# An adaLN block on one core: prologue in another load order, last batch with second homes and its own PSUM banks

## The chip, the cores and the metric

The kernel runs on one core of one Trainium2 chip. The metric is device time in microseconds (us) of one execution; lower is better. Before the change it is 464.82 us, the median of three runs (464.0 to 464.89).

## The reference, cut to what matters

Four batches of 1,024 tokens, 512 wide. A conditioning vector makes six modulation vectors per batch; the block is an attention half and a feed-forward half.

```python
mod = (silu(c) @ wmod).reshape(4, 6, 1, -1)
sa, ca, ga, sb, cb, gb = [mod[:, i] for i in range(6)]      # ga, gb: sign * max(|.|, 0.25)
h = layernorm(x) * (1 + ca) + sa
scores = einsum('hr,bir,bjr->bhij', ones, h @ Wq.T, h @ Wk.T)   # the same for all 16 heads
x = x + ga * (softmax(scores) @ (h @ Wv.T)) @ Wo.T
h = layernorm(x) * (1 + cb) + sb
x = x + gb * (einsum('btd,rde->bte', h, factors) / sqrt(8) + bias)
```

All heads have the same scores, so the kernel multiplies Wv and Wo once into one 512x512 matrix ("wvo"), and sums the eight factors once.

## The kernel before, in words

The 4,096 tokens are 32 tiles of 128 (T = 32), eight per batch. Every product is made in three matmuls (`three`, L461): each operand is split by ScalarE (ACT) into a rounded "hi" part and by VectorE (DVE) into the rest, "lo". SB, CB and so on are the modulation vectors, each made by eight narrow matmuls from its 512x512 piece of `wmod` (`w_part` holds the pieces' parts).

**Prologue.** SP loads Wv, Wo, wmod in four row chunks k each; PE makes wvo (`weights_term`, `weights_last`), the vectors SA and CA between them, then projects the eight tiles of the first batch (`prep_pair`). PE begins with seven fp32 matmuls on zeros (WARMUPS, L672). `scores(0)` and `modulation_columns(1)` stand at the prologue's end.

**Steps.** `step(t)` on every engine handles tile t: PE turns or takes the turned softmax of tile t, projects tile t+8, makes the feed-forward of tile t-3 (`feed_forward`, 12 matmuls of 512 columns), the scores of tile t+2 (4 matmuls), and `attend(t)` (24 matmuls). All but a few tiles turn their softmax without PE: `send_p` writes it to DRAM, `fetch_p` reads it back in quarters, DVE transposes 32x32 blocks (`turn_p`), ACT makes `pt_hi` (`probs_part`), DVE `pt_lo` (`probs_rest`). This is called the P trip below. The normalised x1 goes the same way (`send_x1`, `fetch_x1`, `turn_x1`), then `modulate_x1`, `h2_upper` (ACT) and `h2_rest` (DVE) make the feed-forward's input. After it ACT copies the result out (`ffn_out`), GpSimd (POOL) adds bias, gates and adds it (`add_bias`, `gate_result`, `add_result`), and SP stores pairs of tiles.

**Order.** Every engine runs its own list in program order, and semaphores join them; a waiting instruction holds all behind it on its engine, SP's DMA issues too. The last eight tiles (24 to 31) have no tile to project; their steps are `closing_step` (L909, L1242) on ACT and DVE. There is one home for pt_hi/pt_lo, one for h2, one `ffn` buffer, one output bank `ps_o` for attend and one, `ps_y`, for the feed-forward. After attend(31) come x1 of tile 31, its statistics on DVE, POOL's inverse root, ACT's normalisation, PE's `last_transpose` and the last feed-forward in two column halves.

Of the kernel before, what the change touches and what calls it, by code (L numbers as in the profile page):

```python
# [15 lines left out]
WARMUPS = 7  # L16
# [42 lines left out]
def adaln_block(nc, x, wqk_t, wv, wo_t, factors, bias, c_t, wmod, out):  # L59
# [38 lines left out]
    with ExitStack() as ctx:  # L98
# [26 lines left out]
        rden = sb("rden", [P, 2])  # L125
# [34 lines left out]
        w_hi = [w_parts[i] for i in (0, 1, 0, 1, 4, 1)]  # L160
# [41 lines left out]
        h2_parts_of = [(h2_hi, h2_lo), (h_hi[:, :, 0:P], h_lo[:, :, 0:P])]  # L202
        column_halves = [slice(0, D // 2), slice(D // 2, D)]
        last_banks = [ps_y, ps_o]
# [10 lines left out]
        x_loaded = sem("x_loaded")  # L215
        y_stored = sem("y_stored")
        last_stored = sem("last_stored")
        last_steps = sem("last_steps")
        bias_added = sem("bias_added")
        gate_stored = [sem("ga_stored"), sem("gb_stored")]  # L220
# [4 lines left out]
        weights_hi_done, weights_lo_done = sem("weights_hi_done"), sem("weights_lo_done")  # L225
        w_hi_done = [sem(f"w_hi_done{v}") for v in range(6)]
# [52 lines left out]
        def in_quarters(tile):  # L279

            return tile[:].rearrange("p k (b c) -> p k b c", b=Q)
# [9 lines left out]
        def raw(v, k):  # L291

            if v in (SA, CA):
                return wmod_0[:, k, D * v:D * (v + 1)]
            return (wmod_1 if v < CB else wmod_2)[:, v % 2, k, :]

# [4 lines left out]
        def _(sp):  # L301
# [17 lines left out]
            def load_wmod():  # L319
                for k in range(C):  # L320
                    load_rows(wmod_0, wmod[:, 0:2 * D], k, wmod_loaded)
# [23 lines left out]
            sp.dma_start(probs[:, early:early + C * B], c_t).then_inc(c_loaded, 16)  # L345
            load_v_and_o(0)
            load_wmod()
            load_v_and_o(1)
            load_x(0)
            load_v_and_o(2)  # L350
            load_v_and_o(3)
# [6 lines left out]
            sp.dma_start(f_sum[:], factors[0].rearrange("(c p) n -> p c n", p=P)).then_inc(f0_loaded, 16)  # L358
            load_x(3)
            load_vector(CB)  # L360
            load_vector(GB)
            sp.wait_ge(mod_acc, GA + 1)
            load_x(4)
            load_x(5)
            sp.dma_start(bias_bc[:], bias.partition_broadcast(P)).then_inc(bias_loaded, 16)
# [73 lines left out]
            for t in range(T):  # L439
                if t == 1:  # L440
                    sp.wait_ge(mod_acc, GB + 1)
                    load_x(6)
                step(t)
                if t == 2:
                    load_x(7)
                    store_gate(1, GB)
                if t == 3:
                    spread_gate(1, 0)
            last = PAIRS - 1
            store_pair(last - 1)  # L450
            for half in range(2):
                sp.wait_ge(last_steps, 2 * half + 5)
# [7 lines left out]
        def _(pe):  # L460
# [90 lines left out]
            def attend(t, g, aside=None):  # L551

                pe.wait_ge(v_lo_done, (g >> 2) * TB + TB)
                wait(pe, attn_done, t)
                first = ((g >> 2) & 1) * TB
                for j in range(TB):
                    if j == 3 * TB // 4 and aside is not None:
# [4 lines left out]
                    last = three(ps_o[:], (pt_hi[:, j, :], pt_lo[:, j, :]), v, j == 0, j == TB - 1)  # L562
# [11 lines left out]
            def feed_forward(t, parts=h2_parts_of[0], acc=ps_y, between=None):  # L574
                pe.wait_ge(f_lo_done, C)
                pe.wait_ge(h2_lo_done, t + 1)
                if acc is ps_y:
                    wait(pe, ffn_done, t)
                for k in range(C):
# [5 lines left out]

            def prep_pair(pair, ahead=None, aside=None):

                for u in range(2):
                    transpose_x(2 * pair + u + 1)
                    if u:  # L590
                        pe.wait_ge(h_lo_done, 2 * pair + 2)
# [9 lines left out]
            def step(t, late_x=None, ready=None):  # L601
# [5 lines left out]
                if t < T - TB:  # L607
                    if u:
                        pe.wait_ge(h_lo_done, t + TB + 1)
                        project_qk(g + PB)  # L610
                    if late_x is not None:
                        late_x()
                    project_values(t + TB, u)
                if t > T - TB and scored_in(t) is not None:
                    scores_of(scored_in(t))
                if t >= 3:
                    feed_forward(t - 3)
                if t <= T - TB and scored_in(t) is not None:
# [3 lines left out]
                attend(t, g, transpose_last_but_one if t == T - 1 else None)  # L622
                if scored_last_in(t) is not None:
# [16 lines left out]

            def weights_term(k, i, j):

                pe.wait_ge(weights_hi_done, 2 * k + 2)
                if i:
                    pe.wait_ge(weights_lo_done, 2 * k + 1)
                if j:
                    pe.wait_ge(weights_lo_done, 2 * k + 2)
# [4 lines left out]
            def weights_last(k):  # L652

                pe.wait_ge(weights_lo_done, 2 * k + 2)
# [24 lines left out]
            early_upper(0)  # L679
            early_upper(1)  # L680
            early_rest(0)
            early_upper(2)
            early_rest(1)
            early_upper(3)
            early_rest(2)
            early_rest(3)
            weights_term(1, 0, 0)
            weights_term(1, 1, 0)
            weights_term(1, 0, 1)
            weights_term(2, 0, 0)  # L690
            pe.wait_ge(ident_set, 2)
            pe.wait_ge(rows_done, 2)
            modulation_columns(0, (SA, CA))
            transpose_x(0)
            weights_term(2, 1, 0)
            weights_term(2, 0, 1)
            weights_last(3)
            pe.wait_ge(wqk_lo_done, 1)
# [12 lines left out]
            for t in range(3, T):  # L711
                step(t)
            feed_forward(T - 3)
# [909 lines left out]
```

## Time and profile before

| | us |
|---|---|
| the profiled execution | 464.78 |
| its span (first to last instruction) | 463.0 |
| outside the span | 1.8 |
| PE (matmul) busy | 450.1 (97%) |
| DVE busy | 365.9 (79%) |
| ACT busy | 338.8 (73%) |
| POOL busy | 237.7 (51%) |

A matmul row shows how long one matmul took from start to end (0.39 us for 512 columns), while the next starts before that end. So a PE that looks 97% busy is judged by the distance from start to start, and an idle time printed before a row is about 0.17 us shorter than the stall itself.

### The profile page before, as it was taken

To read this page: it belongs to the slowest core of one execution; us is meant where nothing else is said; L and a number is where in the kernel's file an instruction comes from. 1 tells how busy PE (TensorE), PEld (TensorE's weight loads), DVE (VectorE), ACT (ScalarE), POOL (GpSimd) and SP (SyncE) were. 2 spreads that over 40 slices of the span, in tenths; PEclk is the share of its full clock that TensorE was granted. 3 is DMA by queue.
4 is the path that set the end of the run, shared out by engine and by line. 5 is a ranking of instruction groups with operands and counts; after the bars stand their busy time and mean duration, and the time that the engine had idled before them with its cause. 6 is when DMAs were issued, how large, how long until landed. Compare 5 with 4: busy or idle time off the path is not lost. (4 is left out here: it accounts for less than half of the span.)

```text
span 463.0 us, 7344 instructions
## 1 busy us (share of the span) xinstructions
PE 450.1 (97%) x2114; PEld 365.1 (79%) x2114; DVE 365.9 (79%) x641; ACT 338.8 (73%) x676; POOL 237.7 (51%) x307
## 2 busy tenths in 40 slices
PE   8989999999999999999999999999999999999996
PEld 5768778788888888888888888888888777777674
DVE  5988879678777878789787987798887577887765
ACT  5889777687868777778787786878786566567552
POOL 0347546152555554455565645454644475566662
PEclk9999999999999999999999999999999999999999
DMA  7999999634678365867677366877674237565512
GB/s 288 382 356 218 158 177 170 141 74 132 183 206 271 92 206 159 264 203 241 195 195 228 110 216 190 258 201 245 185 227 115 91 117 227 158 217 180 183 58 91
DMA packets 79160, 88.07 MB, mean 190 GB/s; under 512 B 4872, under 2 KB 55816, under 8 KB 79120
## 3 DMA queue, kind: packets, MB, share of 16 engines
q1 hardware_dynamic: 75168, 80.00, 56.5%
q0 software_dynamic: 3808, 7.34, 9.6%
q8 instruction: 17, 0.28, 0.2%
q10 hardware_dynamic: 144, 0.26, 0.2%
q14 instruction: 23, 0.19, 0.1%
HBM read 53.49 MB, written 34.10 MB: 189 GB/s over the span
## 5 line engine op out<-in xcount | busy, mean ns | idle before, releaser
L1470 POOL TENSOR_SCALAR ve<-mv 128x1 f32<-128x1 f32 x64 | 22.5, 351 | 165.7 <-DVE mv L1173 120.1
L464 PE MATMUL ps_o<-v_lo,pt_hi 128*128 128x512 f32 x256 | 100.2, 391 | 0.9 <-DVE pt_lo L1062 0.9
L466 PE MATMUL ps_o<-v_hi,pt_hi 128*128 128x512 f32 x256 | 99.7, 389 | 0.0
L465 PE MATMUL ps_o<-v_hi,pt_lo 128*128 128x512 f32 x256 | 99.6, 389 | 0.0
L1062 DVE TENSOR_TENSOR h_lo<-h_f,h_hi 128x512 fp32r<-128x512 f32 (+1 forms) x67 | 49.7, 741 | 12.2 <-ACT h_hi L728 11.6
L464 PEld LDWEIGHTS ps_o<-v_lo,pt_hi 128*128 128x128 f32 x256 | 48.0, 188 | 12.9 <-issue 2.9
L466 PEld LDWEIGHTS ps_o<-v_hi,pt_hi 128*128 128x128 f32 x256 | 48.0, 188 | 10.1
L465 PEld LDWEIGHTS ps_o<-v_hi,pt_lo 128*128 128x128 f32 x256 | 48.1, 188 | 9.7
L756 ACT ACTIVATE h_f<-x1b,mod_t 128x128 f32<-128x128 f32 x120 | 53.1, 596 | 2.8 <-DVE x1b L1191 2.5
L464 PE MATMUL ps_y<-f_lo,h_hi 128*128 128x512 f32 (+1 forms) x124 | 48.7, 393 | 2.3 <-issue 1.5
L465 PE MATMUL ps_y<-f_hi,h_lo 128*128 128x512 f32 (+1 forms) x124 | 47.9, 386 | 0.0
L466 PE MATMUL ps_y<-f_hi,h_hi 128*128 128x512 f32 (+1 forms) x124 | 47.9, 386 | 0.0
L1472 POOL TENSOR_TENSOR rstd<-ve,minus_half 128x1 f32<-128x1 f32 x64 | 44.8, 700 | 5.3
L756 ACT ACTIVATE h_f<-xb,mod_t 128x128 f32<-128x128 f32 x80 | 35.4, 593 | 12.9 <-DVE xb L1187 12.8
L464 PE MATMUL ps_v<-wvo_lo,h_hi 128*128 128x512 f32 x112 | 44.3, 396 | 0.0
L465 PE MATMUL ps_v<-wvo_hi,h_lo 128*128 128x512 f32 x112 | 43.8, 391 | 0.0
L1196 DVE STREAM_TRANSPOSE pb<-pb 128x1024 f32<-128x1024 f32 x24 | 29.8, 1241 | 17.6 <-DMA pb<-p_blocks 17.6
L466 PE MATMUL ps_v<-wvo_hi,h_hi 128*128 128x512 f32 x112 | 43.6, 390 | 0.0
L1487 POOL TENSOR_TENSOR ffn<-ffn,bias_bc 128x512 f32<-128x512 f32 x29 | 40.2, 1388 | 5.8 <-ACT ffn L865 5.8
L1497 POOL TENSOR_TENSOR x_ring<-ffn,x_ring 128x512 f32<-128x512 f32 x30 | 38.8, 1293 | 5.2 <-POOL ffn L1493 5.0
L1493 POOL TENSOR_TENSOR ffn<-ffn,gates 128x512 f32<-128x512 f32 x29 | 38.8, 1338 | 4.9 <-issue 4.5
L1121 DVE TENSOR_REDUCE negmax<-ps_s 128x1 f32<-128x1024 f32 x32 | 38.8, 1212 | 2.0 <-PE ps_s L541 1.8
(201 smaller groups left out, 1032.2 us busy)
## 6 DMA issues: line engine op xcount, KB each, us to landing
x_blocks<-xn SPq DMA_DIRECT2D x50, 256.0 KB, 2.7
p_blocks<-probs SPq DMA_DIRECT2D x24, 512.0 KB, 3.6
pb<-p_blocks SPq DMA_DIRECT2D x96, 128.0 KB, 3.2
x_ring<-in_x SPq DMA_DIRECT2D x16, 512.0 KB, 4.6
x1b<-x_blocks SPq DMA_DIRECT2D x30, 256.0 KB, 2.9
result<-x_ring SPq DMA_DIRECT2D x15, 512.0 KB, 3.0
f_sum<-in_factors POOLq DMA_DIRECT2D x14, 512.0 KB, 6.2
xb<-x_blocks SPq DMA_DIRECT2D x20, 256.0 KB, 2.9
```

What stands on the lines that cost most here:

```text
L464: nc.tensor.matmul(acc, a_hi, b_lo, start=first, stop=False)
L465: nc.tensor.matmul(acc, a_lo, b_hi, start=False, stop=False)
L466: return nc.tensor.matmul(acc, a_hi, b_hi, start=False, stop=last)
L756: last = nc.scalar.activation(to[:, k, :].rearrange("p (c b) -> p b c", b=Q), turned[:, k], ACT.Identity, scale=mod_t[:, b, v + 1, k:k + 1 ...
L1062: return nc.vector.tensor_tensor(to, whole, full(hi), ALU.subtract)
L1121: nc.vector.tensor_reduce(negmax[:, t & 3:(t & 3) + 1], ps_s[:], AX_X, ALU.max, negate=True).then_inc(max_done, 1)
L1196: nc.vector.transpose(pb[:, n & 1, :], pb[:, n & 1, :]).then_inc(pb_turned, 1)
L1470: nc.gpsimd.tensor_scalar(ve[:, one], mv[:, u, 1:2], EPS, None, ALU.add).then_inc(ve_done, 1)
L1472: nc.gpsimd.tensor_tensor(rstd[:, one], ve[:, one], minus_half[:], ALU.pow).then_inc(rstd_done, 1)
L1487: nc.gpsimd.tensor_tensor(ffn[:], ffn[:], bias_bc[:], ALU.add).then_inc(biased_done, 1)
L1493: nc.gpsimd.tensor_tensor(ffn[:], ffn[:], gates[:, 1, b & 1, :], ALU.mult).then_inc(gated_done, 1)
L1497: nc.gpsimd.tensor_tensor(tile, ffn[:], tile, ALU.add).then_inc(y_done, 1)
```

## The change

Prologue: the small load of c goes to ACT's queue; Wv/Wo chunk 0 is loaded, rounded and used first, and the wmod chunks are mixed with Wv/Wo chunk 1; x of tile 0 and 1 are two loads; GA, SB and CB get other w_part homes, so CB and x pairs 4 and 5 are loaded without waiting for GA's matmuls; two of Wv's rests go to POOL; the wait on `wqk_lo` moves behind the first projection; `pair_q(0)` and `row(CB)` move up. The warm-up matmuls become eight and 128 wide. Last batch: pt, h2 and ffn get second (and third) homes, attend alternates between ps_qk and ps_o, the feed-forward between ps_y and ps_v, and the order of all five engines is written out tile by tile.

```diff
-WARMUPS = 7
+WARMUPS = 8
...
-        w_hi = [w_parts[i] for i in (0, 1, 0, 1, 4, 1)]
+        w_hi = [w_parts[i] for i in (0, 1, 1, 4, 1, 1)]
...
+        pt_homes = [(pt_hi[:], pt_lo[:]),
+                    tuple(v[:, 0:2, :].rearrange("p s (j i) -> p (s j) i", i=P) for v in (v_hi, v_lo))]
...
+        ffn_homes = [ffn[:], x_ring[:, 0, :]]
...
-        last_banks = [ps_y, ps_o]
+        last_banks = [ps_s[:, 0:D // 2], ps_s[:, D:D + D // 2]]
...
+        def y_bank(t):
+            if t == T - 2:
+                return ps_t[1]
+            return ps_v if t >= late - 3 and t % 2 else ps_y
+
+        def o_bank(t):
+            return ps_qk if t >= late and t % 2 == 0 else ps_o
...
@@ SP @@
-            sp.dma_start(probs[:, early:early + C * B], c_t).then_inc(c_loaded, 16)
...
+            send_p(25)
+            fetch_p(25)
+            send_p(26)
+            send_x1(23, 1)
+            fetch_x1(23, 1)
+            fetch_p(26)
+            send_p(27)
...
+            store_pair(14)
@@ PE @@
-                wait(pe, attn_done, t)
+                wait(pe, attn_done, t if t < late else t - 1)
...
-                nc.tensor.matmul(ps_t[0][0:LO_ROW + B, 0:C * (LO_ROW + B)], no_parts[:, 0, :],
-                                 no_parts.rearrange("p c n -> p (c n)"), start=True, stop=True)
+                nc.tensor.matmul(ps_t[0][:, 0:early], probs[:, 0:P], probs[:, 0:early], start=True, stop=True)
...
-            pe.wait_ge(wqk_lo_done, 1)
             prep_pair(0)
...
+            scores_of(25)
+            transpose_probs(24)
+            feed_forward(21)
+            scores_of(26)
+            attend(24, 12)
+            scores_of(27)
+            feed_forward(22)
+            attend(25, 12)
...
+            attend(31, 15)
+            feed_forward(27)
+            transpose_last_but_one()
+            feed_forward(28)
+            feed_forward(29)
+            last_transpose()
+            feed_forward(30)
+            last_half(0)
+            last_half(1)
@@ ACT @@
-                act.wait_ge(o_acc, t)
+                act.wait_ge(o_acc, t if t <= late else t - 1)
...
-                wait(act, y_done, t)
+                wait(act, y_done, t if t < late - 3 else t - 1)
...
+            h2_upper(22)
+            ffn_out(21)
+            exponentials(26)
+            normalize_x1(23, 1, False)
...
@@ DVE @@
+            gate_next_to_last()
+            add_next_to_last()
+            gate_third_last()
+            gate_half(0)
```

PE around the end of attention: `ps_o` rows are attend(31), `ps_t0` with xn is the transposition of tile 30's x1, `ps_y` the feed-forward that comes next. Before:

```order
L466 MATMUL ps_o<-v_hi,pt_hi 128x512
L470 MATMUL ps_t0<-ident,xn 128x128 [waits x2n_done]
L470 MATMUL ps_t0<-ident,xn 128x128 x3
L464 MATMUL ps_o<-v_lo,pt_hi 128x512
L465 MATMUL ps_o<-v_hi,pt_lo 128x512
L466 MATMUL ps_o<-v_hi,pt_hi 128x512
L464 MATMUL ps_o<-v_lo,pt_hi 128x512
L465 MATMUL ps_o<-v_hi,pt_lo 128x512
L466 MATMUL ps_o<-v_hi,pt_hi 128x512
L464 MATMUL ps_y<-f_lo,h2_hi 128x512 [waits ffn_done,h2_lo_done,f_lo_done]
```

Now, after attend(31) and the feed-forward of tile 27 in ps_v:

```order
L530 MATMUL ps_v<-f_lo,h2_hi 128x512
L531 MATMUL ps_v<-f_hi,h2_lo 128x512
L532 MATMUL ps_v<-f_hi,h2_hi 128x512
L536 MATMUL ps_t0<-ident,xn 128x128 [waits x2n_done]
L536 MATMUL ps_t0<-ident,xn 128x128 x3
L530 MATMUL ps_y<-f_lo,v_hi 128x512 [waits v_lo_done,ffn_done,h2_lo_done,f_lo_done]
```

The transposition left attend(31), and behind attention stand now the feed-forwards of tiles 27 to 30 instead of 29 and 30.

DVE at the end of the prologue (`negmax` is row_max(0), `pb<-ps_o,pb` is row(CB), `v_lo<-ps_t0` the values of tile 6, `mod_t` the columns of SB and CB; pair_q(0) is `qs_lo`). Before:

```order
L1116 CAST qs_lo<-qk_lo 64x256 [waits qk_lo_done]
L1117 CAST qs_lo<-qk_lo 64x256
L1062 TENSOR_TENSOR v_lo<-ps_v,v_hi 128x512 [waits v_hi_done]
L1079 CAST h_hi<-h_f 128x4x128 [waits qk_acc,h_f_done]
L1121 TENSOR_REDUCE negmax<-ps_s 128x1 [waits s_acc]
L1062 TENSOR_TENSOR h_lo<-h_f,h_hi 128x4x128 [waits h_hi_done]
L1062 TENSOR_TENSOR v_lo<-ps_t0,v_hi 128x512 [waits v_hi_done]
L1318 TENSOR_TENSOR pb<-ps_o,pb 4x512 [waits rows_done,low_copied,mod_acc]
```

Now:

```order
L1229 TENSOR_TENSOR v_lo<-ps_v,v_hi 128x512 [waits v_hi_done]
L1246 CAST h_hi<-h_f 128x4x128 [waits qk_acc,h_f_done]
L1288 TENSOR_REDUCE negmax<-ps_s 128x1 [waits s_acc]
L1229 TENSOR_TENSOR h_lo<-h_f,h_hi 128x4x128 [waits h_hi_done]
L1495 TENSOR_TENSOR pb<-ps_o,pb 4x512 [waits rows_done,low_copied,mod_acc]
L1229 TENSOR_TENSOR v_lo<-ps_t0,v_hi 128x512 [waits v_hi_done]
```

qs_lo stands five rows further up, ahead of the last pair's qk, and row(CB) changed places with the values of tile 6.

DVE at the very end (ps_y and ps_v before, ps_t1, ps_v and ps_s now, are feed-forward results; `ffn<-` or `x_ring<-ps_v` is tile 29's gating). Before:

```order
L1181 SCALAR_TENSOR_TENSOR ffn<-ps_y,gates 128x512 [waits y_done,y_acc]
L1445 TENSOR_TENSOR x1b<-x_ring,xb 128x512 [waits h2_f_done,bias_added]
L1135 CAST h2_hi<-h2_f 128x128 [waits h2_f_done]
L1062 TENSOR_TENSOR h2_lo<-h2_f,h2_hi 128x128 [waits h2_hi_done]
```

Now:

```order
L1352 SCALAR_TENSOR_TENSOR probs<-ps_t1,gates 128x512 [waits y_acc,p_out]
L1434 TENSOR_TENSOR x_ring<-probs,x_ring 128x512 [waits last_steps1,bias_added]
L1352 SCALAR_TENSOR_TENSOR x_ring<-ps_v,gates 128x512 [waits y_done,y_acc]
L1352 SCALAR_TENSOR_TENSOR attn<-ps_s,gates 128x256 [waits y_acc]
L1445 TENSOR_TENSOR x_ring<-attn,x1b 128x256 [waits last_steps3,last_steps0]
```

Tile 29's gating stood ahead of the last tile's input parts; now it stands behind the gating of tile 30.

## Rows read from the trace of the kernel before

**Rows 1.** Busy us (instructions) by stage: prologue, middle, last batch.

```profile
0.00:66.00 66.00, 62.03 (x315) 47.25 (x316) 52.59 (x108) 52.41 (x107) 28.29 (x46) 1.00 0.97 267
66.00:368.00 302.00, 301.72 (x1422) 251.01 (x1421) 243.53 (x421) 232.28 (x466) 154.82 (x204) 1.00 0.66 186
368.00:463.00 95.00, 86.36 (x380) 66.82 (x378) 69.80 (x113) 54.08 (x103) 54.56 (x58) 1.00 0.48 151
```

**Rows 2.** PE timeline, last batch.

```profile
362.36 0.39 PE L464 MATMUL ps_o<-v_lo,pt_hi 128*128 128x512 f32 x1
...
368.71 1.03 PE L470 MATMUL ps_t<-ident,probs 128*128 128x128 f32 x8
370.58 0.47 PE L464 MATMUL ps_y<-f_lo,h_hi 128*128 128x512 f32 x1 [0.83 <-ACT ffn L865]
...
392.35 0.47 PE L464 MATMUL ps_y<-f_lo,h_hi 128*128 128x512 f32 x1 [0.58 <-issue]
...
395.53 0.47 PE L464 MATMUL ps_o<-v_lo,pt_hi 128*128 128x512 f32 x1 [0.20 <-DVE pt_lo L1062]
...
449.03 0.47 PE L464 MATMUL ps_y<-f_lo,h_hi 128*128 128x512 f32 x1
...
454.61 0.66 PE L470 MATMUL ps_t<-ident,xn 128*128 128x128 f32 x4 [0.48 <-ACT xn L839]
...
458.25 0.28 PE L464 MATMUL ps_o<-f_lo,h_hi 128*128 128x256 f32 x1
...
459.56 0.28 PE L466 MATMUL ps_o<-f_hi,h_hi 128*128 128x256 f32 x1
```

**Rows 3.** PE timeline, prologue: start, us, operation, idle before and releaser.

```profile
1.10 3.58 PE L673 MATMUL ps_t<-probs 128*36 128x144 f32 x14 [1.10 <-DVE probs L1296]
5.35 0.80 PE L649 MATMUL ps_v<-v_hi 128*128 128x512 f32 x1 [0.68 <-ACT v_hi L728]
...
8.08 0.63 PE L649 MATMUL ps_y<-v_hi,v_lo 128*128 128x512 f32 x1
8.51 0.57 PE L649 MATMUL ps_qk<-v_hi,v_lo 128*128 128x512 f32 x1
...
24.68 0.66 PE L470 MATMUL ps_t<-ident,xn 128*128 128x128 f32 x4 [1.20 <-DVE wqk_lo L1062]
...
59.67 0.47 PE L540 MATMUL ps_s<-k_both,qs_lo 128*128 128x512 f32 x1 [0.55 <-DVE qs_lo L1117]
...
63.94 0.66 PE L503 MATMUL ps_o<-ident,pb 4*128 4x4 f32 x8 [0.37 <-DVE pb L1318]
```

**Rows 4.** Costliest groups of the page: busy us, mean ns, idle before.

```profile
L1121 DVE TENSOR_REDUCE negmax<-ps_s 128x1 f32<-128x1024 f32 x32 | 38.8, 1212 | 2.0 <-PE ps_s L541 1.8
```

**Rows 5.** ACT timeline: softmax numerators of tile 26.

```profile
379.60 1.10 ACT L804 ACTIVATE probs<-ps_s,negmax 128x1024 f32<-128x1024 f32 x1
```

**Rows 6.** DVE timeline: h2 rest, and tile 26's pt_lo.

```profile
390.96 1.29 DVE L1062 TENSOR_TENSOR h_lo<-h_f,h_hi 128x512 fp32r<-128x512 f32 x1
...
394.72 1.26 DVE L1062 TENSOR_TENSOR pt_lo<-pb,pt_hi 128x512 fp32r<-128x512 f32 x2
```

**Rows 7.** DVE timeline: gating of tile 30.

```profile
457.65 0.68 DVE L1181 SCALAR_TENSOR_TENSOR probs<-ps_v,gates 128x512 f32<-128x512 f32 x1
```

**Rows 8.** DVE timeline: the same addition beside a busy and an idle POOL.

```profile
371.10 1.36 DVE L1164 TENSOR_TENSOR x_ring<-attn,x_ring 128x512 f32<-128x512 f32 x1
...
382.18 0.69 DVE L1164 TENSOR_TENSOR x_ring<-attn,x_ring 128x512 f32<-128x512 f32 x1
```

**Rows 9.** POOL timeline beside it, and its last addition.

```profile
372.07 1.53 POOL L1493 TENSOR_TENSOR ffn<-ffn,gates 128x512 f32<-128x512 f32 x1 [0.17 <-issue]
...
453.67 1.27 POOL L1497 TENSOR_TENSOR x_ring<-ffn,x_ring 128x512 f32<-128x512 f32 x1
```

**Rows 10.** DMA issues: KB each, median us from issue to landing.

```profile
result<-x_ring SPq DMA_DIRECT2D x15, 512.0 KB, 3.0
```

**Rows 11.** ACT timeline at the second tile's modulation.

```profile
25.37 0.81 ACT L733 ACTIVATE h_f<-ps_t,mod_t 128x128 f32<-128x128 f32 x2 [1.21 <-PE ps_t L470]
```

More of the change, by code:

```diff
@@ L437, in step @@
                     load_x(g - 2 + 2 * PB)
-            for t in range(T):
+            for t in range(T - TB):
                 if t == 1:
@@ L561, in attend @@
                     v = [part[:, first + j, :] for part in (v_hi, v_lo)]
-                    last = three(ps_o[:], (pt_hi[:, j, :], pt_lo[:, j, :]), v, j == 0, j == TB - 1)
+                    last = three(o_bank(t)[:], [part[:, j, :] for part in pt_of(t)], v, j == 0, j == TB - 1)
                 last.then_inc(o_acc, 1)
@@ L584, in feed_forward, with last_half @@
                 last.then_inc(y_acc, 1)
+            def last_half(half):
+                pe.wait_ge(exp_done, T)
+                for k in range(C):
+                    if half == 0:
+                        pe.wait_ge(last_lo_done, k + 1)
+                    last = three(last_banks[half], [part[:, k, :] for part in h2_of(T - 1)],
+                                 [part[:, k, column_halves[half]] for part in (f_hi, f_lo)], k == 0, k == C - 1)
+                last.then_inc(y_acc, 1)
             def prep_pair(pair, ahead=None, aside=None):
@@ new lines, in _ @@
+            row_max(25)
+            pair_q(13)
+            turn_x1(22)
+            add_x(23)
+            probs_rest(24, 0)
+            invert_sum(24, 0)
+            x1_stats(23, 1)
+            row_max(26)
+            probs_rest(24, 1)
+            invert_sum(25, 1)
+            h2_rest(22)
+            invert_sum(26, 0)
+            gate_attention(24, 0, 3)
+            turn_p(25)
+            add_x(24)
+            probs_rest(25, 0)
+            x1_stats(24, 0)
+            row_max(27)
@@ new lines, in _ @@
+            probs_rest(25, 1)
+            pair_q(14)
+            turn_p(26)
+            turn_x1(23)
+            invert_sum(27, 1)
+            probs_rest(26, 0)
+            gate_attention(25, 1, 3)
+            row_max(28)
+            probs_rest(26, 1)
+            h2_rest(23)
+            add_x(25)
+            x1_stats(25, 1)
+            turn_p(27)
+            gate_attention(26, 0, 3)
+            add_x(26)
+            probs_rest(27, 0)
+            row_max(29)
+            turn_x1(24)
@@ new lines, in _ @@
+            x1_stats(26, 0)
+            probs_rest(27, 1)
+            turn_p(28)
+            pair_q(15)
+            h2_rest(24)
+            probs_rest(28, 0)
+            gate_attention(27, 1, 3)
+            add_x(27)
+            row_max(30)
+            x1_stats(27, 1)
+            turn_x1(25)
+            probs_rest(28, 1)
+            invert_sum(28, 0)
+            turn_p(29)
+            row_max(31)
+            probs_rest(29, 0)
+            probs_rest(29, 1)
+            gate_attention(28, 0, 3)
```

590 lines of the change are left out of this document (382 added, 208 removed).

## The prediction

> **What bounds the kernel now.** I began with the busy table by stage [rows 1]. Its columns are the stretch's length, then busy time of PE, PE's weight loads, DVE, ACT and POOL, then the granted clock. PE is busy 301.72 of 302 us in the middle and nobody else is near, so the middle is PE's own work and the change hardly touches it. Time can be won at the ends only: the prologue's PE idles 4.0 of 66 us, the last batch's 8.6 of 95. The granted clock is full in the mean of each stage (1.00). Since matmuls overlap, I count PE from start to start. Pace: 28 matmuls of 512 columns lie between 362.36 and 368.71 [rows 2], 0.2268 us each; a transposition takes (1.03 - 0.28)/7 = 0.107, a matmul of 256 columns (459.56 - 458.25)/11 = 0.119 [rows 2].
>
> Prologue, read in the PE timeline [rows 3]: the first real matmul starts at 5.35; PE idles 1.20 before 24.68, 0.55 before 59.67, 0.37 before 63.94. A printed idle time plus about 0.17 is the stall from start to start: 1.37, 0.72, 0.54.
>
> Last batch: from 368.71 to the last matmul's start at 459.56 plus 0.12 are 90.97 us. In them stand 336 matmuls of 512 columns (ten feed-forwards of 12, six scores of 4, eight attends of 24), 16 transpositions and 24 matmuls of 256 columns: 76.2 + 1.7 + 2.9 = 80.8. **10.2 us are lost**, in some twenty places, of which [rows 2] shows four: the wait for the single ffn buffer at 370.58 (0.83), for the h2 rest at 392.35 (0.58, released by something that the view calls issue), for pt_lo at 395.53 (0.20), for tile 31's normalisation at 454.61 (0.48). The others repeat these, once or twice per tile; and the scores wait for the numerators of the tile before, since ACT takes these late.
>
> **The change, last batch (-8.8).** Each cause gets an answer. ffn waits: two homes, and the feed-forward alternates banks. Numerators: ACT now takes them ahead of normalising and modulating. h2: a second home, and each feed-forward stands a tile later, so its input is ready a whole tile early. pt_lo: here I compare a trip with a distance. The trip of tile 26 takes 1.2 for row_max [rows 4] and from the start of its numerators at 379.60 [rows 5] to attend at 395.53 [rows 2] 15.9, together 17.1. DVE spends 390.96 to 394.72 [rows 6], 3.7, on h2_rest, the gating and adding of x1 and its statistics ahead of pt_lo; the new order puts these behind it. That leaves 13.4. The distance that PE gives: between scores(25) and attend(25) now stand 8 transpositions and 56 matmuls, 0.86 + 12.7 = 13.6; for the other tiles 76 or 80 matmuls, 17.2 or 18.1. So tile 25 fits by 0.2, the others fit, but their slack also pays for the SP queue: `send_x1` and `fetch_x1` of tile 23 stand ahead of `fetch_p(26)`, and the x1 trip's two transfers can hold it. My hand schedule leaves tile 26 about 0.6. Behind attend(31) three feed-forwards (27, 28, 29; 8.2 us) instead of one and a half cover the chain of tile 31's x1, which takes 5.6 now, from the first matmul behind attend(31) at 449.03 to its transposition at 454.61 [rows 2]. So all 10.2 could go; margins this thin will let some places slip. I take 1.4 of residue (chosen: two or three slips of 0.5 to 0.7), bounds 0 (every margin holds) and 5 (six or seven attends each late by 0.6 to 0.7). 10.2 - 1.4 = 8.8.
>
> **The tail (+1.0).** Before, the last matmul ends near 459.8 and the span at 463.0, 3.2 later. Now DVE gates and adds tile 30 (0.68 [rows 7] and 0.69, the undisturbed addition of [rows 8]), then gates tile 29 (0.68), 2.15 with the gaps between; POOL adds tile 29 in 1.27 [rows 9] and its pair is stored, 512 KB in 3.0 [rows 10], plus 0.5 of hand-overs: the end is X + 7.0, where X is the end of feed-forward 30 on PE. The other path is X + 24 x 0.119 + 3.2 = X + 6.0, as before. So the third-last tile, done early, is now last to leave: +1.0. If POOL's other queue work overlaps less than I think it is +1.5; if the store takes less for lying alone, 0.
>
> **Prologue (-1.8).** (a) Start: the warm-up row is 1.10 plus seven fp32 matmuls in two passes each, 14 rows, 3.58 [rows 3], 0.24 a pass. Eight of them end at 1.10 + 16 x 0.24 = 4.94 at the earliest, and v_hi, which released 5.35, is now loaded first, so the start comes 0.1 to 0.4 sooner. (b) The 1.37 stall before 24.68 waited for wqk_lo; this wait moves behind the first projection. But ACT idled 1.21 before its 25.37 modulation [rows 11], and in that gap now stand wqk_hi's rounding and a fourth GA chunk, for which I take 0.5 apiece (two small pieces of the modulation are 0.81 in that row): ACT is late next. (a) and (b) together: bounds 0 (ACT holds it all) and 1.8 (both through); I take 0.7. (c) 59.67: pair_q(0) stands five rows earlier, and PE waits next for the k rests: 0.6 of 0.72. (d) 63.94: row(CB) ahead of the values of tile 6: 0.5 of 0.54; these values are needed only by attention. CB and x pairs 4 and 5 arriving earlier is worth nothing, as no PE wait in the prologue names them. 0.7 + 0.6 + 0.5 = 1.8.
>
> **Sum.** The profiled execution took 464.78, 0.04 below the median of 464.82, so the sum stands for the median. 464.78 - 8.8 + 1.0 - 1.8 = 455.2.
>
> **A rule against the change.** The row first: the same addition on DVE took 1.36 at 371.10, beside POOL's additions and gatings, and 0.69 at 382.18, when POOL was done with its tile [rows 8, 9]. The new order packs POOL's chain and DVE's pt_lo and x1 work into the same stretch, and with no stall to hide in, 0.67 for one such instruction per tile on seven tiles is 4.7 us lost: nearly rival B. The Trainium skill (SBUF — State Buffer, "Who interferes with whom") says that a DVE instruction with two SBUF inputs contends with a GpSimd instruction that reads SBUF, and that the one that comes second is blocked until the first is through. The rows agree in size (about twice 0.69, while POOL's took 1.53 instead of 1.27). By this rule alone the sum would be about 459.9; by the rows I expect the collision mostly where DVE has slack (DVE is busy 69.8 of 95 [rows 1]), hence 455.2.
>
> **Rivals.**
> A (0.60), as above; its own range is 453.3 to 457.5.
> B (0.17): the P trip is late at every tile, through SP's order or through DVE beside POOL. Speaks for it: the slack of 0.2 to 0.6; against it: tiles 27 to 31 have 3.8 or more before SP's part. Seven attends late by 0.6 each, 4.2: 459.4.
> C (0.08): ACT swallows the prologue's gain and two late slips come: 455.2 + 1.8 = 457.0.
> D (0.10): PE's clock rises earlier. The matmuls at 8.08 and 8.51 are 0.43 apart [rows 3] against the pace of 0.2268, so PE runs at its lower level, 1.2 GHz, till 8.9 or so; the eighth and wider warm-ups put work in front. At most 8 matmuls x 0.2 = 1.6 would be won, but loads and ACT are late next, and about 0.6 passes through: 454.6. The Trainium skill (TensorE: Matmul & The Clock Gate, "What's actually happening") says that throttled is the default state and activity releases it; the slow first matmuls agree.
> E (0.03), slower: SP's queue is in order. `fetch_x1(23)` waits for its blocks to land, behind it `fetch_p(26)`, behind that DVE's turn, pt_lo and attend. If each of seven tiles comes L late, the time is 455.2 + 7 L; it is slower than 464.8 from L = 1.4. At L = 1.6, about half of the 3.0 that a transfer takes [rows 10], it is 466.4.
> F (0.02): the new order does nothing, since another wait (PE's own issue) set the stalls: 464.8.
>
> **Numbers.** A measurement here tells 0.2%, 0.9 us, from no change. 455.2 is A's. The range 452.9 to 459.5 takes in A, C, D and the middle of B: below it less than a tenth (no residue and more of the start), above it E, F and half of B. Faster: all but E and F and rounding, 0.95; same 0.02; slower 0.03.
>
> **What would show it.** After: first real matmul at 5.0 to 5.3; no idle of 1 us near 24, but one of ACT's making of 0.3 to 0.8; nothing of 0.5 before scores(0) and the SB/CB columns; the last batch's PE stretch near 82 us with at most five stalls, all under 0.7; the span's end 7 us behind feed-forward 30, on a store of tile 28 and 29. The forecast is wrong if a new wait stands in front of attend at every tile (B, E: its releaser pt_lo, with fetch_p late on SP), if spacing at the start falls to 0.23 before 8 us (D), or if POOL, with 54.6 us busy of 95, becomes what ffn waits for.

## The result, and the profile after

The changed kernel takes 462.82 us (median of 20 executions, 459.86 to 467.93) beside 465.34 for the kernel before (20 executions): a ratio of 0.9941, with a 95% interval of 0.9921 to 0.9961, or 2.7 us saved. The two medians stand 2.5 us apart, and the ratio differs a little because it leaves out the one execution (467.93) that is over 1.5% slower than the fastest. Forecast were 455.2 us and 9.6 us saved, so the direction was right and the size far off, outside the stated range.

Two numbers have to be kept apart. The execution that was profiled took 460.14 us, 4.6 less than the profiled one of before (464.78). The median over all executions saves only 2.7. So the forecast, made against one trace, has 4.9 us to explain in the trace and some 2 us more in what a typical execution does.

Busy time by stage of the changed kernel (length, PE, weight loads, DVE, ACT, POOL, granted clock):

```profile
0.00:66.00 66.00, 63.79 (x327) 49.12 (x328) 53.78 (x110) 53.54 (x111) 30.61 (x48) 1.00 0.97 272
66.00:366.00 300.00, 299.33 (x1412) 249.17 (x1411) 243.98 (x417) 230.76 (x462) 154.03 (x203) 1.00 0.64 186
366.00:458.30 92.30, 84.67 (x381) 68.72 (x379) 76.58 (x113) 52.34 (x103) 55.61 (x58) 0.96 0.50 156
```

Against [rows 1], PE's idle time in the prologue fell from 4.0 to 2.2 us, but the last batch still has 7.6 us without PE (4.5 of them behind the last matmul), and its granted clock is no longer 1.00. DVE is busy for 76.6 us instead of 69.8, on the same 113 instructions. The list of who PE waited for (total us, times, longest) says where, and that it is something new:

```profile
PE ps_s L530 <- DVE v_lo L1229: 1.8, 2, 0.9
PE ps_qk L530 <- DVE pt_lo L1229: 1.1, 2, 0.7
PE ps_t L766 <- DVE probs L1486: 1.1, 1, 1.1
PE ps_t L536 <- ACT xn L851: 0.4, 1, 0.4
PE ps_t L569 <- DVE pb L1495: 0.4, 1, 0.4
```

The waits for ffn, numerators and h2 are gone. The longest one stands in the last two matmul groups of the program. Here is PE's timeline from the end of feed-forward 30 on:

```profile
447.08 0.39 PE L532 MATMUL ps_t<-f_hi,h_hi 128*128 128x512 f32 x1
447.32 0.36 PE L530 MATMUL ps_s<-f_lo,v_hi 128*128 128x256 f32 x1
...
448.78 0.38 PE L530 MATMUL ps_s<-f_lo,v_hi 128*128 128x256 f32 x1 [0.86 <-DVE v_lo L1229]
...
450.32 0.39 PE L530 MATMUL ps_s<-f_lo,v_hi 128*128 128x256 f32 x1 [0.92 <-DVE v_lo L1229]
...
453.36 0.41 PE L532 MATMUL ps_s<-f_hi,v_hi 128*128 128x256 f32 x1
```

DVE makes the last tile's parts, two operations for each of four 128x128 pieces:

```profile
445.89 1.28 DVE L1229 TENSOR_TENSOR v_lo<-h_f,v_hi 128x128 fp32r<-128x128 f32 x1
447.10 1.30 DVE L1313 CAST v_hi<-h_f 128x128 fp32r<-128x128 f32 x1
448.43 0.29 DVE L1229 TENSOR_TENSOR v_lo<-h_f,v_hi 128x128 fp32r<-128x128 f32 x1
448.64 1.30 DVE L1313 CAST v_hi<-h_f 128x128 fp32r<-128x128 f32 x1
449.97 0.29 DVE L1229 TENSOR_TENSOR v_lo<-h_f,v_hi 128x128 fp32r<-128x128 f32 x1
450.18 0.22 DVE L1313 CAST v_hi<-h_f 128x128 fp32r<-128x128 f32 x1
```

The same CAST takes 1.30 us twice and 0.22 once, the same subtraction 1.28 and then 0.29. In the trace of before all four casts took 0.22 to 0.23 and all four subtractions 0.29; the first of them:

```profile
455.79 0.23 DVE L1135 CAST h_hi<-h_f 128x128 fp32r<-128x128 f32 x1 [2.22 <-ACT h_f L1051]
```

POOL beside DVE, in the new trace:

```profile
445.73 1.30 POOL L1759 TENSOR_TENSOR x_ring<-x_ring 128x512 f32<-128x512 f32 x1
446.98 1.34 POOL L1750 TENSOR_TENSOR ffn<-ffn,gates 128x512 f32<-128x512 f32 x1
448.49 1.36 POOL L1759 TENSOR_TENSOR x_ring<-ffn,x_ring 128x512 f32<-128x512 f32 x1 [0.18 <-POOL ffn L1750]
```

Each long DVE row ends 0.1 us behind a POOL row (those end at 447.0, 448.3 and 449.9), and the short ones start where POOL is between two operations or done. Behind PE's idle times of 0.86 and 0.92 us, at about 451.5, the granted clock falls; the table of the last stretches shows it:

```profile
445.00:450.00 5.00, 3.53 (x17) 2.52 (x15) 4.63 (x6) 1.28 (x4) 4.67 (x4) 1.00 0.28 107
450.00:454.00 4.00, 3.46 (x18) 3.12 (x18) 3.76 (x8) 0.00 (x0) 1.07 (x1) 0.69 0.17 66
```

From 451.65 on the halves follow each other at 0.21 us instead of 0.119, the lower level of 1.2 GHz. The last matmul starts 0.8 later for it than in the second trace below, where the clock stayed up.

DVE and POOL after the pieces:

```profile
450.64 0.68 DVE L1352 SCALAR_TENSOR_TENSOR probs<-ps_t,gates 128x512 f32<-128x512 f32 x1
...
453.16 1.32 DVE L1445 TENSOR_TENSOR x_ring<-attn,x1b 128x256 f32<-128x256 f32 x1
454.40 0.41 DVE L1352 SCALAR_TENSOR_TENSOR attn<-ps_s,gates 128x256 f32<-128x256 f32 x1
454.92 0.42 DVE L1445 TENSOR_TENSOR x_ring<-attn,x1b 128x256 f32<-128x256 f32 x1
```

```profile
452.93 1.27 POOL L1759 TENSOR_TENSOR x_ring<-x_ring 128x512 f32<-128x512 f32 x1 [3.08 <-DVE x_ring L1352]
```

From 445.26 to 455.34 DVE has work without a pause, and it takes up the second column half at 454.40, 0.6 after PE's last matmul has ended. So at the end the kernel waits for DVE and not for PE.

**Balance of the two profiled executions.** Three marks divide them: attend(0) starts at 69.54 and now 67.28; attend(23) at 362.36 and now 360.47; feed-forward 30 ends (X in the prediction) at 456.49 and now 447.31; the spans end at 463.0 and 458.3. So the prologue gives 2.3 us (forecast 1.8), the middle takes back 0.4 (forecast 0), the last batch up to X gives 7.3 of the 8.8, and the end from X to the last instruction grows from 6.5 to 11.0 us: +4.5 instead of +1.0. That adds up to the 4.7 between the spans.

### The profile page after: what moved, and what is told of

It is laid out like the page before. It is cut to its first block, busy times and chain, and to the rows that moved or that the text cites. A ratio compares the mean times of both kernels' runs of the same rounds, so it can differ in the third digit from the quotient of the medians.

```text
span 458.3 us, 7372 instructions
## 1 busy us (share of the span) xinstructions
PE 447.8 (98%) x2116; PEld 367.0 (80%) x2116; DVE 374.3 (82%) x639; ACT 336.6 (73%) x676; POOL 240.3 (52%) x309
## 4 chain that ended last, share of the span: by engine, by line
PE 69%; DMA 14%; DVE 6%; ACT 4%; issue 3%; SPq 2%; POOL 1%; DVEq 0%; ACTq 0%; POOLq 0%
PE ps_o L532 8%; PE ps_o L530 8%; PE ps_o L531 8%; PE ps_v L530 5%; PE ps_v L531 5%; PE ps_v L532 5%; DMA x_blocks<-xn 5%; PE ps_y L530 4%; PE ps_y L531 4%; PE ps_y L532 4%; DMA p_blocks<-probs 3%; DMA xb<-x_blocks 3%; PE ps_s L606 2%; PE ps_qk L530 2%; PE ps_s L607 2%
## 5 line engine op out<-in xcount | busy, mean ns | idle before, releaser
L532 PE MATMUL ps_o<-v_hi,pt_hi 128*128 128x512 f32 x192 | 74.7, 389 | 0.0
L531 PE MATMUL ps_o<-v_hi,pt_lo 128*128 128x512 f32 x192 | 74.7, 389 | 0.0
L530 PE MATMUL ps_o<-v_lo,pt_hi 128*128 128x512 f32 x192 | 74.7, 389 | 0.0
L1229 DVE TENSOR_TENSOR h_lo<-h_f,h_hi 128x512 fp32r<-128x512 f32 x57 | 41.9, 736 | 10.7 <-ACT h_hi L837 10.5
L530 PEld LDWEIGHTS ps_o<-v_lo,pt_hi 128*128 128x128 f32 x192 | 36.0, 188 | 7.7
L531 PEld LDWEIGHTS ps_o<-v_hi,pt_lo 128*128 128x128 f32 x192 | 36.0, 188 | 7.5
L913 ACT ACTIVATE probs<-ps_s,negmax 128x1024 f32<-128x1024 f32 x32 | 35.5, 1108 | 8.8 <-DVE negmax L1288 8.5
L837 ACT ACTIVATE v_hi<-ps_v 128x512 fp32r<-128x512 f32 x28 | 16.8, 598 | 25.0 <-PE ps_v L532 25.0
L530 PE MATMUL ps_y<-f_lo,h_hi 128*128 128x512 f32 x88 | 34.5, 392 | 0.1
L531 PE MATMUL ps_y<-f_hi,h_lo 128*128 128x512 f32 x88 | 34.3, 390 | 0.0
```

Source lines behind the costliest of these rows:

```text
L530: nc.tensor.matmul(acc, a_hi, b_lo, start=first, stop=False)
L531: nc.tensor.matmul(acc, a_lo, b_hi, start=False, stop=False)
L532: return nc.tensor.matmul(acc, a_hi, b_hi, start=False, stop=last)
L913: nc.scalar.activation(to, source, ACT.Exp, bias=negmax[:, t & 3:(t & 3) + 1], accum_out=rowsum[:, t & 3:(t & 3) + 1]).then_inc(exp_done, 1)
L1229: return nc.vector.tensor_tensor(to, whole, full(hi), ALU.subtract)
```

## The experiments

Each kernel was timed beside the kernel before on the same chip; ratios are to that kernel, with 95% intervals, and the time is a median.

**The changed kernel once more.** No edit.

> The changed kernel once more, to get a second trace of it. If the spread of its executions (459.9 to 467.9) comes from transfers that reach attention late in the last batch, a slower trace shows longer idle times of PE in front of attends 26 to 31 (0.84, 0.36 and 0.60 in the first trace) and the same prologue and end. If it comes from elsewhere, the last batch is as before and PE has lost time ahead of it. Time: 460 to 466, ratio to the kernel before 0.990 to 0.998.

462.79 us, ratio 0.9951 (0.9919 to 0.9984). The second trace is of a longer execution, with a span of 463.1. Its list of PE's waits:

```profile
PE ps_qk L530 <- DVE h_lo L1229: 3.4, 3, 1.7
PE ps_qk L530 <- DVE pt_lo L1229: 2.1, 2, 1.8
PE ps_s L530 <- DVE v_lo L1229: 1.8, 2, 0.9
```

The end is the same to a tenth: X to the end of the span 11.0 us again, the same two waits for v_lo. But the clock did not fall in it, and the last matmul starts 5.2 us behind X instead of 6.0. The same stretch as in the last row of that table, counted from X:

```profile
454.75:458.75 4.00, 2.52 (x18) 2.27 (x18) 3.76 (x8) 0.00 (x0) 1.07 (x1) 1.00 0.17 66
```

So the lower clock of the first trace cost PE 0.8 us and the kernel nothing. Two other things differ. First, the wait for h_lo (projection of queries and keys in the middle) is 3.4 us where it was 0.3, and attend(0) to attend(23) takes 296.8 instead of 293.2. Second, attend(26) waits 1.8:

```profile
392.69 0.47 PE L530 MATMUL ps_qk<-v_lo,pt_hi 128*128 128x512 f32 x1 [1.78 <-DVE pt_lo L1229]
```

SP's own timeline explains it:

```profile
378.61 0.38 SPq L435 DMA_DIRECT2D p_blocks<-probs  x1
379.11 0.43 SPq L406 DMA_DIRECT2D x_blocks<-xn  x1
384.70 0.34 SPq L411 DMA_DIRECT2D x1b<-x_blocks  x1
385.14 1.80 SPq L443 DMA_DIRECT2D pb<-p_blocks  x4
```

`fetch_x1(23)` could only be issued at 384.70, once the x1 blocks sent at 379.11 had landed (384.54), and `fetch_p(26)` stands behind it. The order is only a part of this: the p blocks sent at 378.61 landed at 383.88 themselves, 5.3 us after their issue (3.4 in the first trace), so by my estimate the order holds `fetch_p(26)` back by 1.2 us. Both mechanisms that were expected for a slower trace hold: late transfers in the last batch, and lost time ahead of it, where the larger part lies.

**The prologue's part alone**, on the kernel before: every edit up to step 0 on all engines, of which three stand here.

```diff
-WARMUPS = 7
+WARMUPS = 8
...
-        w_hi = [w_parts[i] for i in (0, 1, 0, 1, 4, 1)]
+        w_hi = [w_parts[i] for i in (0, 1, 1, 4, 1, 1)]
...
-            pe.wait_ge(wqk_lo_done, 1)
             prep_pair(0)
```

> The kernel before with the prologue's part of the change alone. My theory: the prologue works as forecast (1.9 us by the first trace) and the last batch gives too little. Then the ratio is 0.994 to 0.997. If the prologue's gain is given back in the middle, where projections and loads meet other transfers, the ratio is 0.998 to 1.001.

465.79 us, ratio 1.001 (0.9982 to 1.0039). Its trace has attend(0) at 67.34, as early as the changed kernel, and attend(23) at 364.46, 2.1 us later than in the trace of before. The prologue's gain is there at 67 us and not at 464 us: the second forecast of the two.

**POOL held back at the end.**

```diff
             gate_result(27, 3)
+            pool.wait_ge(last_lo_done, C)
             add_bias(28)
```

> The changed kernel, with POOL waiting for the last tile's parts on DVE before it adds the bias of tile 28. Theory of the port: DVE's conversions of tile 31 took 1.3 us instead of 0.25 because POOL's additions stood beside them; held back, they are 0.22 to 0.29 again, PE ends near 450.3 on the scale of the first trace instead of 453.6, POOL finishes later but the whole ends 2 to 3 us sooner: ratio to before about 0.989. Rival, a slow read of h2_f or the semaphores between pieces: the pieces stay at 1.3 us and the time is 1 to 3 us longer, because POOL's four operations start late.

463.54 us, ratio 0.9956 (0.9928 to 0.9983). The mechanism came out as the port theory says, the time did not (0.989 was forecast). The trace is of an execution of 468.66 us, 5 above the median, and is read for its end alone. DVE's pieces with POOL standing still, and POOL's start behind them:

```profile
453.19 0.23 DVE L1313 CAST v_hi<-h_f 128x128 fp32r<-128x128 f32 x1 [1.89 <-ACT h_f L969]
453.45 0.29 DVE L1229 TENSOR_TENSOR v_lo<-h_f,v_hi 128x128 fp32r<-128x128 f32 x1
...
455.56 1.29 POOL L1744 TENSOR_TENSOR ffn<-ffn,bias_bc 128x512 f32<-128x512 f32 x1 [3.12 <-DVE v_lo L1229]
```

All eight pieces are 0.22 to 0.30 now, and PE's last matmul starts 2.8 us behind X instead of 6.0. But POOL's remaining five operations now end at 462.7, 7.5 behind X, and the store comes after that: X + 11.6. The 3.3 us that PE won went into POOL's queue. (In this trace PE also ran at the lower clock from 258 to 261, behind a wait of 1.9 us for h_lo and far from the edit.)

**The last tile's input in PSUM.**

```diff
+        last_wholes = [ps_qk, ps_o, ps_y, ps_qk]
...
-                nc.scalar.activation(h2_f[:, k, :], ps_t[0][:, P * k:P * (k + 1)], ACT.Identity,
+                nc.scalar.activation(last_wholes[k][:, 0:P], ps_t[0][:, P * k:P * (k + 1)], ACT.Identity,
...
-                nc.vector.tensor_copy(hi, h2_f[:, here, :]).then_inc(last_hi_done, 1)
+                nc.vector.tensor_copy(hi, whole).then_inc(last_hi_done, 1)
```

> The changed kernel, with the last tile's modulated input written to PSUM banks that are free, so DVE reads one operand of each piece there and POOL may run beside it. Theory of the port: pieces at 0.2 to 0.35 us with POOL busy, PE ends about 3.3 us earlier at the full clock, and the end is then set by POOL's queue and the store of tiles 28 and 29: 3 to 3.5 us gained, ratio to before about 0.987. Rival (the pieces are slow of themselves): ratio 0.994 as the changed kernel.

459.46 us, ratio 0.9878 (0.9841 to 0.9914). The pieces read PSUM, and run at full speed beside POOL:

```profile
450.85 0.29 DVE L1317 CAST v_hi<-ps_o 128x128 fp32r<-128x128 f32 x1
451.17 0.29 DVE L1232 TENSOR_TENSOR v_lo<-ps_o,v_hi 128x128 fp32r<-128x128 f32 x1
451.38 0.28 DVE L1317 CAST v_hi<-ps_y 128x128 fp32r<-128x128 f32 x1
```

```profile
450.58 1.29 POOL L1763 TENSOR_TENSOR x_ring<-x_ring 128x512 f32<-128x512 f32 x1
451.84 1.28 POOL L1754 TENSOR_TENSOR ffn<-ffn,gates 128x512 f32<-128x512 f32 x1
...
455.04 1.48 POOL L1763 TENSOR_TENSOR x_ring<-x_ring 128x512 f32<-128x512 f32 x1
```

X to the end of the span is 8.5 instead of 11.0 (2.5 won in the trace), and the clock stays up. The intervals of this kernel and of the changed one, timed on the same chip, do not overlap. The end now hangs on POOL's last addition, which ends 4.35 behind X; the store of the pair and the two stores of tile 31 follow it in SP's queue.

**The kernel before once more.** No edit.

> The kernel before once more, for a second trace. The traces with the new prologue lose 4.1 to 4.4 us against it between attend(0) and attend(23), in front of project_qk at 151, 204, 231 and 256, where its own trace lost 0.6. Theory that the new prologue is the cause of it: the second trace of before loses again under 1 us there and attend(23) starts at 362 to 363. Rival, that these stalls come and go with the transfers of an execution or a chip, whatever the prologue: it loses 2 to 4 us there and attend(23) starts at 364 to 367.

One execution, 466.28 us. attend(23) starts at 363.91, between the two forecasts. Attend(0) to attend(23) takes 294.5, against 292.8 in the first trace. So part of the middle's loss comes and goes without the new prologue.

**The last batch's part alone**, on the kernel before: all homes, banks and orders of the last batch, the prologue of before.

```diff
-            for t in range(T - TB, T):
-                closing_step(t)
+            pair_q(13)
+            probs_part(24, 0)
+            exponentials(25)
...
```

> The kernel before with the last batch's part of the change alone. If the prologue's gain is given back in the middle, this is as fast as the changed kernel: ratio to before 0.993 to 0.996. If the prologue's 2 us are really in the total, it is 0.997 to 1.000.

463.05 us, ratio 0.9946 (0.9919 to 0.9972), against 0.9941 and 0.9951 with the new prologue. The last batch is the whole of the measured gain.

**The loads of x behind the fetches.**

```diff
+                if not u and 2 <= g - 1 < PAIRS - 2 * PB + 2:
+                    sp.wait_ge(y_stored, 16 * (g - 2))
+                    load_x(g - 3 + 2 * PB)
                 if 1 <= t < T - 1:
                     send_x1(t - 1, 1 - u)
...
-                if u and 2 <= g < PAIRS - 2 * PB + 2:
-                    sp.wait_ge(y_stored, 16 * (g - 1))
-                    load_x(g - 2 + 2 * PB)
```

> The changed kernel, with each 512 KB load of x from tile 14 on issued behind the fetch of xb and of p instead of right ahead of them. Theory: the load slows the fetch of xb from 3.0 to 4 or 5 us (as rows with a load in front show) and this makes PE wait in front of project_qk. Then these waits (3.4 us in the second trace) fall under 1 us, and the ratio is 0.987 to 0.991. Rival, the late x itself or another transfer makes the wait: ratio 0.994 to 1.000.

A miss: 482.9 us, ratio 1.0343 (1.0298 to 1.0388). The waits for h_lo rose to 14.9 us in 7 places. An x that comes three transfers later is late for its statistics and all that hangs on them. It says that x has no slack in the middle, and nothing on whether its load disturbs the fetch beside it.

**fetch_p(26) ahead of fetch_x1(23).**

```diff
             send_x1(23, 1)
+            fetch_p(26)
             fetch_x1(23, 1)
-            fetch_p(26)
```

> The changed kernel, with fetch_p(26) on SP ahead of fetch_x1(23). In its two traces PE waited 0.84 and 1.94 us for pt_lo of tile 26, as SP stood at fetch_x1(23) until x1's blocks had landed (issued at 379.11, landed at 384.70 in the slower trace). Theory of SP's order: the wait at attend(26) goes, 0.8 to 1.9 us sooner, ratio to before 0.990 to 0.993. Rival, the p blocks land no earlier: as the changed kernel, 0.994.

460.99 us, ratio 0.9904 (0.9869 to 0.994), 1.8 us below the 462.79 of the changed kernel, though the intervals overlap and the two were timed on different chips. The p blocks are fetched before the x1 blocks are waited for, and attend(26) waits 0.52 from start to start, where it was 0.84 and 1.94:

```profile
378.86 1.75 SPq L443 DMA_DIRECT2D pb<-p_blocks  x4
380.80 0.34 SPq L411 DMA_DIRECT2D x1b<-x_blocks  x1
```

Against the first trace of the changed kernel that is 0.3 us at this place; where the rest of the 1.8 comes from is not shown.

**Three repairs together**: the PSUM homes, this order, and tiles 28 and 29 stored singly.

```diff
-            store_pair(14)
+            sp.wait_ge(y_done, T - 3)
+            sp.dma_start(out_pairs[last - 1][:, 0], x_ring[:, 2 * TB - 4, :]).then_inc(y_stored, 16)
...
+            act.wait_ge(y_done, T - 2)
+            act.dma_start(out_pairs[PAIRS - 2][:, 1], x_ring[:, 2 * TB - 3, :]).then_inc(last_stored, 16)
```

> The changed kernel with three repairs: the last tile's input in PSUM banks, fetch_p(26) ahead of fetch_x1(23), and tile 28 and tile 29 stored singly, tile 29 from ACT's queue. Sum of the single effects: 0.9942 (changed kernel), about 0.006 for PSUM, 0.004 for the order of fetches, 1.2 us (0.0025) for the stores: ratio to before 0.982. The trace should show feed-forward 30's end plus 7.0 to 7.3 us as the span's end. If the end is PE's or POOL's in another way, the span still ends 8.4 us behind it and the ratio is 0.985.

458.87 us, ratio 0.9846 (0.9801 to 0.9892). The span ends 7.3 us behind X, the number that was forecast; the ratio is a little above the sum of single effects, within its interval. In its trace PE waits 2.4 us for h_lo in the middle again.

**The three repairs with the prologue of before.**

> The same three repairs, with the prologue of before. If the middle gives back the prologue's 2 us, the ratio is that of the kernel beside it (within 0.003). If the prologue counts in full, it is 0.0045 higher.

457.83 us, ratio 0.9819 (0.9775 to 0.9864): not slower than with the new one, though the intervals are 0.009 wide. Its trace is of an execution of 462.96 us, 5 above the median.

**Five more warm-up matmuls.**

```diff
-WARMUPS = 8
+WARMUPS = 13
```

> The three repairs and the new prologue, with five more warm-up matmuls, which hold back PE alone by 5 x 0.48 = 2.4 us; loads, rounding and the other engines start as they do now. If the middle waits for loads and transfers that do not start with PE, most of the 2.4 is absorbed: ratio within 0.002 of the kernel with 8 warm-ups. If PE's place in time is what the end follows, it is 0.005 higher.

460.17 us, ratio 0.9881 (0.985 to 0.9912). Inconclusive: the ratio is 0.0035 above that of the kernel with eight, between the two forecasts, and the intervals overlap. The first real matmul came at 5.70 instead of 4.93, 0.8 later and not 2.4, and attend(0) 0.7 later.

**Small loads of x in the middle**, with either prologue.

```diff
-                sp.dma_start(x_ring[:, bass.ds(slot, 2), :], x_pairs[pair]).then_inc(x_loaded, 16)
+                if pair < 2 * PB:
+                    sp.dma_start(x_ring[:, bass.ds(slot, 2), :], x_pairs[pair]).then_inc(x_loaded, 16)
+                else:
+                    sp.dma_start(x_ring[:, bass.ds(slot, 2), 0:32], x_pairs[pair][:, :, 0:32]).then_inc(x_loaded, 16)
```

> The kernel with the three repairs and the new prologue; the loads of x from tile 16 on bring only 32 of 512 columns (the rest of the input is stale, so results of later tiles are not the reference's). Theory: the 512 KB loads stand in the way of the fetches of xb, so PE waits in front of project_qk. Then the waits at 150 to 256 go, the stretch from attend(0) to attend(23) is at most 293.0 us (it was 292.8 to 299.4 in the traces so far) and the time is 3 to 4 us below that of the three repairs. Rival, these waits come from the stores, the exchange of softmax blocks or DVE: the stretch stays at 295 to 298.

> The same with the prologue of before. If the loads in the middle swallow the new prologue's lead, then without them the lead of 2.0 us is seen in full: this kernel is 0.004 to 0.005 slower in ratio than the one beside it. If it is not slower, the lead is lost by something else in the middle.

455.69 us, ratio 0.9797 (0.9755 to 0.984), and 457.75 us, ratio 0.982 (0.9785 to 0.9855). All waits of PE for h_lo in the middle are gone in both traces, and no line of either list names h_lo. The list of the first begins so:

```profile
PE ps_t L771 <- DVE probs L1496: 1.1, 1, 1.1
PE ps_y L535 <- ACT ffn L1000: 0.5, 1, 0.5
PE ps_t L541 <- ACT xn L856: 0.4, 1, 0.4
```

Attend(0) to attend(23) takes 293.4 and 292.5 us, near the best of the full kernels; the first is 0.4 above the bound that was forecast. Its median is 3.2 us below that of the three repairs with full loads, with overlapping intervals. With the prologue of before, small loads bring nothing: 0.982 against 0.9819. Between the two, the lead of the new prologue at attend(0) was 1.6, and the medians stand 2.1 apart, while the intervals of their ratios overlap.

## Why the prediction was wrong

Against the profiled execution the forecast is 4.9 us off: the tail took 3.5 more than forecast, the last batch gave 1.5 less and the middle took back 0.4, while the prologue gave 0.5 more. The 2.7 us between that execution and the median come on top.

**What bounds the kernel.** Right in the trace: PE judged start to start, 10.2 us lost in the last batch, gains at the ends only. Wrong in what was left unsaid: one trace of before showed a middle with 0.6 us of loss, and the prediction took "the middle is PE's own work" as a fact of the kernel. Other executions lose 1 to 7 us there. Attend(0) to attend(23) over the traces took 292.8, 294.5, 295.2 and 297.1 with the old prologue and 293.2, 296.8, 297.1, 299.4, 297.1, 293.4, 298.2 and 296.4 with the new one.

**The tail (+1.0).** This is the step that failed. The prediction has two paths to the end, "the end is X + 7.0, where X is the end of feed-forward 30 on PE" and "The other path is X + 24 x 0.119 + 3.2 = X + 6.0, as before." Both let DVE be free at X. Neither has in it the eight operations that make the last tile's parts, though these stand on DVE ahead of both: in the trace of before they ended 1.2 behind X, and its tail measures 6.5 and not 6.0. Now they end 3.4 behind X and the span 11.0.

The pieces are longer because DVE makes them beside POOL, and the forecast had seen that collision: it priced one addition per tile, from [rows 8], and put the rule aside, "where DVE has slack". At the end DVE has none. Before, POOL was idle from 454.9 on and the pieces ran undisturbed; the new order leaves POOL with six full-width operations behind x1 of tile 31 (441.5 to 449.9 in the trace), since every feed-forward comes a tile later. The eight pieces take 5.5 us from 445.26 on instead of the 1.9 from 455.79 on that they took before. That POOL is the cause is shown from two sides: standing still, it lets the same instructions run at 0.22 to 0.30, and with PSUM as their source they run at 0.28 and 0.29 beside it. The Trainium skill (SBUF — State Buffer, "Who interferes with whom") states three things: two SBUF inputs contend with a POOL read, copies and casts can enter modes that contend, and an instruction with at most one SBUF input outside those modes does not. All three agree with these rows, as far as 128x128 pieces go.

Measured from X in the two first traces, the +4.5 adds up so: the pieces end 2.2 later; tile 29's gating stands in front of the first half's (0.6); the first half's addition takes 1.32 instead of 0.42 beside POOL's at 452.93 (0.9); and the last store takes 2.5 from issue to landing instead of 1.7, on SP behind the store of the pair (0.8). The path that the forecast put at X + 7.0 is late as well: the store of the pair lands at X + 9.9.

PE's own losses are not in this sum. Its two waits for v_lo (1.8 us) and the lower clock (0.8) delay its last matmul, but DVE comes to the halves later still. Five traces have this end: the two of the changed kernel and those of the last batch alone, of the late loads and of fetch_p(26) first. The last matmul starts 5.2 behind X in the three in which the clock stayed up, 6.0 and 6.6 in the two in which it fell, and the span ends 11.0 behind X in all five.

With the three repairs the span ends at X + 7.3, but that it is near 7.0 is luck: tile 29, stored by itself, lands at X + 6.5, and the last to land is the second half of tile 31 at X + 6.8, on the path that was put at 6.0.

**The last batch (-8.8).** The mechanism was right and the size somewhat off: from attend(23) to X the trace lost 9.9 us before and 2.6 now, 7.3 won. The residue of 1.4 was 2.6. Tile 25 with its slack of 0.2 did not wait. Tiles 26 (0.84), 29 (0.36) and 30 (0.60) did. The slack of tile 26 was set at 0.6 by a schedule with transfers of one length, and their length is what varies: 1.9 us of wait in the second trace. In part that is rival E's mechanism, SP held by fetch_x1(23), at one tile instead of seven; moving one line takes that part away. The rule that the forecast put aside was priced at 4.7 us for this stretch. Of the 6.8 us by which DVE's busy time rose in the last batch, 4.4 are in the pieces and the one addition of the end, and 2.4 are spread over the batch; how much of PE's 2.6 comes from them no run shows.

**The prologue (-1.8).** Right in size (2.3 us at attend(0) in the first trace, 1.4 to 2.7 in the others, against the first trace of before). PE starts at 4.88, 0.06 before the earliest time given. The stall at 24.68 left 0.25 and 0.55 in its place, and the columns and scores(0) no longer wait as they did. The sign that was given for rival D came, though: PE's first real matmuls stand 0.23 apart, not 0.43.

```profile
5.22 0.39 PE L741 MATMUL ps_o<-v_hi 128*128 128x512 f32 x1
5.45 0.40 PE L741 MATMUL ps_y<-v_hi 128*128 128x512 f32 x1
```

The clock is granted in full from 4.4 us on in this trace and by 6.4 in every trace with the new prologue; with the old one it came at 8.9 to 10.1 in four traces and at 4.6 in the fifth. By attend(0) little of it is left, which is D's own condition ("loads and ACT are late next"): the old prologue with full clock from 4.6 on has attend(0) at 69.39 beside 69.54, and the new one alone, with full clock only from 6.4 on, at 67.34 beside 67.28. But in the total it is worth nothing that can be measured: alone 1.001 (at most 0.8 us by the interval), and 0.9846 against 0.9819 with the repairs.

**Where the prologue's gain goes.** Shown: it is there at attend(0), it is not there in the medians, and most of the loss lies in front of project_qk in the middle. With the 512 KB loads of x cut to a sixteenth, both traces are free of these waits. That is weaker evidence than it looks, since three of the twelve other traces had at most 0.3 us of them too, and since with the old prologue the small loads do not change the median. It agrees with single transfers: in the second trace of the changed kernel the fetch of xb issued at 142.08 behind a load was turned only at 147.35, where 3.0 us is usual.

```profile
147.35 0.71 DVE L1358 STREAM_TRANSPOSE xb<-xb 128x512 f32<-128x512 f32 x1 [3.43 <-DMA xb<-x_blocks]
```

Not shown: why the new prologue should make the loss greater. The old one averages 294.9 us over four traces and the new one 296.4 over eight, with single traces from 292.8 to 299.4. That is 1.5 of the 2.2, but the spread is four times as wide as the difference, and 297.1 and 299.4, the longest of each list, come from the two executions that were 5 us above their medians. With small loads the lead seems to come back (2.1 us of medians, overlapping intervals). It stays open.

**Range.** The range of 452.9 to 459.5 took its upper end from seven late attends. No rival priced the end of the program beyond +1.5, and none a middle that takes something back, so the case that came was in none of them, though one of its parts, the early clock, was D's.

## What to carry to other kernels

When an order is made tighter, list for the last stretch what every engine still has to do behind the last dependent tile, start each path where its engine is really free, and set the helper's operations in time beside the critical small ones. If they are DVE and POOL on SBUF, give the critical ones a PSUM source or take POOL's work away from them: that was worth 3.3 us of median here, more than the whole change had brought. Holding POOL back is no cure where its own queue ends the kernel.

A trace is one execution. Compare its stalls in several executions before a term rests on "no loss there"; and follow a gain early in the program to its end, for here 2 us at attend(0) were no gain in the median.

On a queue that works in order, put the fetch that is needed first ahead of any entry that waits for a landing.

## What was not expected of the hardware

A 128x128 CAST from SBUF took 1.30 us beside POOL's 128x512 operation and 0.22 without, so the small instruction paid for POOL's long one in full; with PSUM as the source it took 0.28 to 0.29 beside POOL. The same two waits of 0.9 us of PE were followed by a granted clock of 1.2 GHz in two of the five traces that have them and by none in three, and the end of the program came at the same distance from X in all. And fetches of 256 KB with a 512 KB load issued 2 us before them took between 2.8 and 5.3 us from issue to DVE's turn; the one at 142 took 3.7 in one execution of the changed kernel and 5.3 in the other.
